# Latent attention of one Trainium2 kernel: from bf16 stacks of parts to fp32 strips of 32 partitions

## The reference, cut to what matters

```python
D_MODEL, N_HEADS, N_KV, HEAD_DIM, D_LAT = (128, 8, 2, 128, 32)
scale = HEAD_DIM ** (-0.5)
q = (x @ wq).reshape(Bq, Tq, N_KV, N_REP, HEAD_DIM)
k_lat = (x @ wk_down).reshape(Bq, Tq, N_KV, D_LAT)
v_lat = (x @ wv_down).reshape(Bq, Tq, N_KV, D_LAT)
k = jnp.einsum('bkhl,ld->bkhd', k_lat, wk_up)
v = jnp.einsum('bkhl,ld->bkhd', v_lat, wv_up)
scores = jnp.einsum('bqhrd,bkhd->bhrqk', q, k) * scale
scores = jnp.where(causal, scores, jnp.finfo(scores.dtype).min)
probs = jax.nn.softmax(scores, axis=-1)
y = jnp.einsum('bhrqk,bkhd->bqhrd', probs, v)
return y.reshape(Bq, Tq, N_HEADS * HEAD_DIM) @ wo
```

## Time and profile before

| what | us |
|---|---|
| runs of the kernel | 1942.96, 1944.66, 1948.3 |
| median | 1944.66 |
| profiled execution, span | 1933.1 |
| PE busy | 1601.7 (83%) |
| DVE busy | 1180.5 (61%) |
| POOL busy | 818.4 (42%) |
| ACT busy | 786.5 (41%) |
| latent stage, from first projection to last add | 1362.5 to 1846.6 |

### The profile page before, as it was taken

How to read it: one execution, slowest core, us unless ns; L and a number is a source line. 1 busy time by engine, 2 the same in 40 slices (tenths; PEclk the granted TensorE clock), 3 DMA queues, 4 the chain that set the end, 5 groups by cost and what they waited for, 6 DMA issues and landing times.

```text
span 1933.1 us, 25832 instructions
## 1 busy us (share of the span) xinstructions
PE 1601.7 (83%) x8863; PEld 807.4 (42%) x8863; DVE 1180.5 (61%) x2315; ACT 786.5 (41%) x1031; POOL 818.4 (42%) x987
## 2 busy tenths in 40 slices
PE   4766699758999899999799789989545898988779
PEld 2222466412333333332466567766212333333256
DVE  5887633578788787883333333342355878897951
ACT  2222233343565565667333344444212343334433
POOL 2224646464554635455463644000001577456900
PEclk8788699867999999999799999979656898889979
DMA  4000000151000303000000000000143000000000
GB/s 139 1 0 0 1 1 0 59 121 29 2 2 12 41 3 51 2 2 1 1 1 0 0 1 0 0 1 0 49 117 96 1 1 1 1 1 1 1 1 22
DMA packets 31585, 36.86 MB, mean 19 GB/s; under 512 B 8606, under 2 KB 24703, under 8 KB 31362
## 3 DMA queue, kind: packets, MB, share of 16 engines
q1 hardware_dynamic: 27906, 29.29, 6.4%
q10 hardware_dynamic: 3520, 6.29, 1.6%
q0 software_dynamic: 64, 0.00, 0.0%
HBM read 26.10 MB, written 8.91 MB: 18 GB/s over the span
## 4 chain that ended last, share of the span: by engine, by line
PE 61%; DVE 16%; DMA 7%; SPq 3%; issue 2%; ACT 2%; ACTq 0%; DVEq 0%
PE PS L943 9%; PE PS L1355 9%; PE PS L931 9%; PE PS L1304 8%; PE PS L1374 8%; DVE sb_latent_acc L1462 3%; DMA sb_rope_K<-rope_parts 3%; PE PS L1723 3%; PE PS L1741 3%; SPq L1629 2%; DVE sb_latent_mp L1538 2%; DMA latent_parts<-sb_latent_parts 2%; DVE sb_rope_mp L1538 2%; DVE sb_latent_rec L1568 1%; PE PS L1735 1%
## 5 line engine op out<-in xcount | busy, mean ns | idle before, releaser
L1538 DVE TENSOR_REDUCE sb_rope_mp<-PS 128x1 f32<-128x512 f32 (+3 forms) x560 | 345.0, 669 | 76.5 <-PE PS L1308 36.9
L1418 ACT ACTIVATE sb_rope_PT<-PS 128x1024 f32<-128x1024 f32 (+3 forms) x320 | 273.3, 895 | 223.0 <-PE PS L1359 121.7
L1462 POOL TENSOR_TENSOR sb_latent_acc<-sb_latent_acc,sb_latent_PT 128x1536 f32<-128x1536 f32 (+3 forms) x72 | 223.2, 3101 | 72.4 <-ACT sb_latent_PT L1418 68.8
L1418 ACT ACTIVATE sb_latent_PT<-PS 128x1024 f32<-128x1024 f32 (+3 forms) x160 | 140.2, 895 | 243.3 <-PE PS L1359 80.9
L995 DVE SCALAR_TENSOR_TENSOR sb_X<-PS,sb_gates,sb_X 128x128 f32 (+1 forms) x320 | 90.1, 344 | 241.3 <-PE PS L943 241.2
L1304 PE MATMUL PS<-sb_rope_K,sb_rope_Q 96*128 96x512 bf16 (+3 forms) x640 | 211.7, 371 | 30.2 <-ACT sb_rope_V L1399 18.3
L1538 DVE TENSOR_REDUCE sb_latent_mp<-PS 128x1 f32<-128x512 f32 (+3 forms) x280 | 174.3, 666 | 46.2 <-PE PS L1304 32.5
L576 POOL TENSOR_SCALAR sb_pbelow<-sb_pa,sb_ptrial 128x512 f32<-128x512 f32 x124 | 197.0, 1599 | 6.4
L583 POOL TENSOR_TENSOR sb_pbelow<-sb_pbelow 128x1024 f32<-128x1024 f32 (+1 forms) x248 | 181.7, 733 | 19.6
L931 PE MATMUL PS<-sb_HT,sb_w 128*128 (+1 forms) x384 | 182.3, 612 | 3.6 <-DVE sb_seed L514 1.9
L1355 PE MATMUL PS<-sb_rope_Q,sb_rope_K 99*128 99x512 bf16 (+3 forms) x640 | 179.4, 352 | 1.4 <-ACT sb_rope_PT L1418 0.9
(11 more groups left out here) (291 smaller groups left out, 2438.7 us busy)
## 6 DMA issues: line engine op xcount, KB each, us to landing
latent_parts<-sb_latent_parts SPq DMA_DIRECT2D x36, 128.0 KB
sb_rope_Q<-rope_parts SPq DMA_DIRECT2D x9, 384.0 KB
rope_parts<-sb_rope_parts SPq DMA_DIRECT2D x24, 128.0 KB, 2.4
sb_rope_tab<-in_rotation SPq DMA_DIRECT2D x1, 2048.0 KB, 8.6
sb_rope_K<-rope_parts SPq DMA_DIRECT2D x6, 256.0 KB
sb_latent_Q<-latent_parts ACTq DMA_DIRECT2D x2, 768.0 KB
sb_latent_Q<-latent_parts SPq DMA_DIRECT2D x1, 1536.0 KB, 19.1
sb_rope_Q<-rope_parts ACTq DMA_DIRECT2D x6, 192.0 KB
```

The costliest lines, as they stand in the source:

```text
L1418: s.activation(self.PT[:, u % 2, 2 * p:2 * p + 2, q0:CH], k.PS[:, 2 * p:2 * p + 2, q0:CH], ACT.Exp, scale=self.scale).then_inc(self.exps[p ...
L1462: eng.tensor_tensor(acc, acc, new, ALU.add).then_inc(self.added[who], 1)
L1538: v.tensor_reduce(self.mp[:, n % 2, kc, heads[0]:heads[-1] + 1, i], k.PS[:, bank, 0:len(heads) * w].rearrange("p (h k) -> p h k", h=len(he ...
```

## The change

A new stage `StripHeads` replaces `CausalHeads` for latent attention; rotary attention keeps the old one.

- The four heads of a quad lie on partitions 0, 32, 64, 96 (32 rows each: a strip) of Q and K, which are fp32. The projection itself puts them there: for K by weights repeated four times (`wkrep`, made by two POOL copies in LaterWeights). There are four projections per chunk. ACT copies Q, DVE copies K. No parts, no constants, no scratch tensor and no load remain.
- Scores and maxima are fp32 matmuls over the 32 rows of a strip. An item of maxima is one head (320 items in place of 280), in the order of strips 2, 3, 0, 1. Masks stay bf16 over all rows and come first. The negated maxima are added by a bf16 matmul of ones with three rows of each strip.
- POOL splits the negated maxima, PE turns them with four transposes, ACT copies them into negT. No DMA.
- The chunk is the outer loop, the quad the inner one. The rate is 5.0, without a steady share.
- PT has three buffers, acc two. Of the units of a chunk every third (kj = 0, 3, 6, ...) has its row sums made by PE (item "part", four matmuls into a ring bank, added to S by DVE), the others are added by POOL alone, all four heads in one instruction of up to 2048 columns.
- At the chunk end PE sums acc, DVE adds it to S; a DMA gathers the four rows into 128 x 16, DVE takes the reciprocal, a DMA puts it back, PE spreads it over each strip ("den"), DVE multiplies, PE projects, DVE adds.
- The constants grow by 128 columns.

The core of the diff:

```diff
+        for i in range(2):
+            g.tensor_copy(k.wkrep[:, i, :, :], k.wkv[:, 0, 32 * i:32 * i + 32].rearrange("p (a l) -> p a l", a=1)
+                          .broadcast_to([P, 4, 32])).then_inc(self.ready, 1)
...
+class StripHeads(Stage):
...
+    R = 3
+    AHEAD = 3
+    PTS = 3
+    NQ = 2
+    NS = 3
+    D = 32
...
+        self.seq = [(c, g) for c in range(NC) for g in range(self.NQ)]
+        self.units = [(n, kj) for n, (c, g) in enumerate(self.seq) for kj in range((c + 1) * TPC)]
+        self.first = [self.units.index((n, 0)) for n in range(len(self.seq))] + [len(self.units)]
...
+    def pe_sums(self, kj):
+        return kj % 3 == 0
+    def chunk_maxima(self, n):
+        c, g = self.seq[n]
+        return [("max", n, i, kc, j) for i in range(TPC) for kc in range(c + 1) for j in (2, 3, 0, 1)]
...
+            late = max(min(d, np.ceil(d - self.rate * max(0, first - self.AHEAD - u))) for first, d in due)
+            return int(min(len(items), max(late, 0)))
...
+            rests[end + 2].append(("sum", n))
+            relays[end + 5].append(("reciprocals", n))
+            rests[end + 7].append(("den", n))
+            rests[end + 8].append(("out", n))
...
+            a, b = (len(mine) + 3) // 4, (len(mine) + 1) // 2
+            if u < total:
+                plan.append((u, "scores0"))
+            plan += ring(mine[:a])
+            if u < total:
+                plan.append((u, "scores1"))
+            plan += ring(mine[a:b])
+            if 1 <= u <= total:
+                if self.pe_sums(self.units[u - 1][1]):
+                    plan.append((None, ("part", u - 1)))
+                plan.append((u - 1, "weighted"))
+            plan += [(u, it) for it in relays[u]]
+            plan += ring(mine[b:])
+            for it in rests[u]:
+                if it[0] == "turn":
+                    plan.append((u, ("split", it[1])))
+                plan.append((None, it))
+        return plan
...
+    def pe_scores(self, pe, u, p):
+        k = self.k
+        n, c, g, kj, q0 = self.unit(u)
+        if p == 0 and kj == 0:
+            self.emptied(pe, ("turn", n))
+        if u:
+            pe.wait_ge(self.exps[p], u)
+        diag = kj >= c * TPC
+        pair = (2 * p, 2 * p + 1)
+        if diag:
+            for j in pair:
+                pe.matmul(k.PS[:, j, q0:q0 + P], k.identb[:, :], k.mask_kq[:, :], start=True, stop=False,
+                          skip_group_check=True)
+        for j in pair:
+            strip = slice(32 * j, 32 * j + 32)
+            pe.matmul(k.PS[:, j, q0:CH], self.K[strip, g, kj * P:(kj + 1) * P],
+                      self.Q[strip, g, c * CH + q0:(c + 1) * CH], start=not diag, stop=False, skip_group_check=True)
+        for j in pair:
+            rows = slice(32 * j, 32 * j + 3)
+            pe.matmul(k.PS[:, j, q0:CH], k.onesb[rows, :], self.negT[rows, n % 2, q0:CH], start=False, stop=True,
+                      skip_group_check=True).then_inc(self.scores[p], 1)
+    def pe_weighted(self, pe, u):
+        k = self.k
+        n, c, g, kj, q0 = self.unit(u)
+        if kj == 0 and n:
+            pe.wait_ge(self.moved, n)
+        for p in range(2):
+            pe.wait_ge(self.exps[p], u + 1)
+        for j in range(4):
+            ins = pe.matmul(k.PS[32 * j:32 * j + 32, 4, q0:CH], self.V[:, kj, g, :], self.PT[:, u % self.PTS, j, q0:CH],
+                            start=(kj == 0), stop=(kj == (c + 1) * TPC - 1))
+        ins.then_inc(self.weighted, 1)
+    def pe_item(self, pe, item, bank):
+        k, kind = self.k, item[0]
+        if kind == "max":
+            _, n, i, kc, j = item
+            c, g = self.seq[n]
+            strip = slice(32 * j, 32 * j + 32)
+            w = CH if kc < c else (i + 1) * P
+            q0 = c * CH + i * P
+            if kc == c:
+                pe.matmul(k.PS[:, bank, w - P:w], k.identb[:, :], k.mask_qk[:, :], start=True, stop=False,
+                          skip_group_check=True)
+            return pe.matmul(k.PS[:, bank, 0:w], self.Q[strip, g, q0:q0 + P], self.K[strip, g, kc * CH:kc * CH + w],
+                             start=kc < c, stop=True, skip_group_check=True)
...
+        if kind == "part":
+            u = item[1]
+            n, c, g, kj, q0 = self.unit(u)
+            for p in range(2):
+                pe.wait_ge(self.exps[p], u + 1)
+            for j in range(4):
+                ins = pe.matmul(k.PS[32 * j:32 * j + 32, bank, q0:CH], k.ones_col, self.PT[:, u % self.PTS, j, q0:CH],
+                                start=True, stop=True)
+            return ins
...
+    def act_exps(self, s, u):
+        k = self.k
+        n, c, g, kj, q0 = self.unit(u)
+        if u >= self.PTS:
+            s.wait_ge(self.weighted, u - self.PTS + 1)
+            s.wait_ge(self.added, self.pool_adds(u - self.PTS + 1))
+        for p in range(2):
+            s.wait_ge(self.scores[p], 2 * (u + 1))
+            s.activation(self.PT[:, u % self.PTS, 2 * p:2 * p + 2, q0:CH], k.PS[:, 2 * p:2 * p + 2, q0:CH], ACT.Exp,
+                         scale=self.scale).then_inc(self.exps[p], 1)
...
+    def pool_add(self, g, u):
+        n, c, quad, kj, q0 = self.unit(u)
+        if self.pe_sums(kj):
+            return
+        if kj == 1 and n >= 2:
+            self.filled(g, ("sum", n - 2))
+        if self.pool_adds(u):
+            g.wait_ge(self.added, self.pool_adds(u))
+        for p in range(2):
+            g.wait_ge(self.exps[p], u + 1)
+        new, acc = self.PT[:, u % self.PTS, :, q0:CH], self.acc[:, n % 2, :, q0:CH]
+        if kj == 1:
+            g.tensor_copy(acc, new).then_inc(self.added, 1)
+        else:
+            g.tensor_tensor(acc, acc, new, ALU.add).then_inc(self.added, 1)
+    def pool_split(self, g, ch, n):
+        part = lambda r: self.negp[:, n % 2, :, :].rearrange("p i (j r) -> p i j r", r=32)[:, :, :, r]
+        neg, rest = self.neg[:, n % 2, :, :], self.rest[:, n % 2, :, :]
+        g.wait_ge(self.zeroed, 1)
+        g.wait_ge(self.negated, n + 1)
+        if n >= 2:
+            self.filled(g, ("turn", n - 2))
+        ch(g.tensor_copy(part(0), neg))
+        ch(g.tensor_tensor(rest, neg, part(0), ALU.subtract))
+        ch(g.tensor_copy(part(1), rest))
+        g.tensor_tensor(part(2), rest, part(1), ALU.subtract).then_inc(self.neg_split, 1)
...
+            a = StripHeads(k, "latent", ln, 5.0)
```

More of the change, by code:

```diff
@@ L98, in __init__ @@
         self.den_rope = self.cst[:, 3 * P:4 * P]
+        self.den_strip = self.cst[:, 15 * P:16 * P]
         self.ones_col = self.cst[:, 4 * P:4 * P + 32]
@@ L116, in bank @@
         return self.PS[:, b, 0:cols]
-N_CST = 5 + 8 + 2
+N_CST = 5 + 8 + 2 + 1
 class NormMemory:
@@ L290, in __init__ @@
         k.wc = sb("wc", [P, 8, 32])
+        k.wkrep = sb("wkrep", [P, 2, 4, 32])
         k.wy = sb("wy", [P, 2, P])
@@ L447, in tensor @@
         pe.wait_ge(s.ready, 1)
-        pe.wait_ge(self.ready, 4)
+        pe.wait_ge(self.ready, 6)
         n = 0
@@ L1881, in constants @@
     c[:, 14 * P:15 * P] = np.where(r[:, None] > r[None, :], MASKED, 0.0)
+    c[:, 15 * P:16 * P] = (r[:, None] // 32 == r[None, :] // 32) & (r[:, None] % 32 == 0)
     c[:, CST_ORDER:] = 8 - np.arange(8)
@@ L1987, in latent_attention @@
             ln = norm()
-            qb = [(0, 0, 0, 2), (0, 64, 0, 1), (1, 0, 0, 3)]
-            kb = [(0, 0, 0, 1), (0, 32, 0, 2), (1, 0, 2, 1), (1, 32, 1, 1), (1, 64, 0, 1)]
-            sources = [(k.wc[:, 4 * g:4 * g + 4, :].rearrange("p h l -> p (h l)"), None) for g in range(2)]
-            a = CausalHeads(k, "latent", ln, 2, sources + [(k.wkv[:, :, :].rearrange("p a l -> p (a l)"), None)], (qb, kb), 96, 1,
-                            k.wkv[:, 1, :], 2, 32, float(P ** -0.5), k.wy, d["latent_parts"], False, True, 4.5)
+            a = StripHeads(k, "latent", ln, 5.0)
             with ExitStack() as arena:
@@ L2042, in scratch @@
     d["rope_parts"] = nc.dram_tensor("rope_parts", (2, 16, 3 * 8, T), BF16).ap()
-    d["latent_parts"] = nc.dram_tensor("latent_parts", (3, 4, 3 * 32, T), BF16).ap()
 def kernel(**inputs):
```

284 lines of the change are left out of this document (added).

## The result

The kernel after takes 2154.09 us (median of four runs, 2127.62 to 2165.42), the kernel before 1946.24 us beside it: ratio 1.1018, 95% interval 1.0944 to 1.1092. The ratio and its interval are of the fast executions, without the slowest of the four after. The forecast was 1916, with a range up to 1995. The profiled execution after took 2127.62 us, the lowest of the four, span 2125.6.

The account below looks back on a forecast made before the run. It took TensorE, gapless in mid-stage units, and 111 us of preparing as the bound. First scores at 1413 plus 392 gave 1805, closing 12.5 gave 1817.5, 29 us earlier: 1944.66 - 29 + 0.3 = 1916 us, range 1860 to 1995.

Parts of the forecast that it names:

- a granted clock of 0.5 in the strips: Strip products: listed sign that the forecast is wrong; the forecast itself expected clock 0.9 at the first scores.
- the rival of 1945 us: Whole stage: preparation 48 us shorter, middle 48 us longer (full unit 5.7 us, missed handovers and lower clock); chance 0.06.
- the sum: Stage from first scores to last units: full units with maxima 5.0 us, diagonal ones, chunk ends, last units; together 392 us.
- Preparation: Before first scores: parts and reloads go, maxima begin at 1383.7 us, first scores at 1413 instead of 1473.6.
- Do strips overlap?: Score products on row strips: a pair of heads overlaps, 0.86 us, 1.07 with negated maxima; 2.13 without overlap.
- The rival of no overlap, 2197 us: Row strips never overlap: a full unit takes 9.9 us, 281 us added; chance 0.12.
- Products start only one after the other: Rival on strip products: no half passes a waiting one, full unit 6.05 instead of 5.0 us, total 1981; chance 0.15.
- VectorE and GpSimd: Beside TensorE in full units: GpSimd adds of 2048 columns 4.6 us, reductions 0.69 us each, both hidden.
- full units have maxima waiting for reductions: Full units: three banks fill, so the fourth maximum waits for the first's VectorE reduction, to 1.8 us; unit 5.0.
- The last units: Units without maxima at the stage's end: 3.2 us each, set by GpSimd and handover.
- The end: After the last weighted group: closing steps take 12.5 us, against 10.5 before.
- 60 us gained: Preparation: first scores at 1413 us instead of 1473.6; bounds 48 to 70 us.

Follow-up runs that it names:

- e6: Kernel after with only the diagonal blocks' maxima taken over all 128 rows instead of one strip, masks kept (values not the reference's): 1962.29 us.
- e5: Kernel after without the mask products before the diagonal maxima: 1933.03 us (ten runs), ratio to before 0.9936.
- e3: Kernel after with VectorE reducing only 128 columns of each maximum: 2149.1 us.
- e1: Kernel after with all maxima over 128 rows instead of a 32-row strip (values are sums over four heads): 2053.37 us.
- e4: Kernel after with maxima taken from bf16 copies of Q and K, one pass instead of two, scores still fp32: 1926.91 us, ratio to before 0.988.
- e9: Kernel after reordered only: where two diagonal maxima follow each other, both masks are issued first, then both products: 2071.2 us.
- e10: e4 (bf16 maxima) with the order of e9 (masks issued in pairs): 1885.48 us, ratio to before 0.9705.
- e7: e4 (bf16 maxima) without the masks before the maxima: 1839.04 us, ratio to before 0.9464.
- e11: e7 with the planner's rate 6.0 in place of 5.0, six maxima a unit: 1865.09 us, ratio to before 0.9602.
- e12: Kernel after with masks left out of the 39 maxima up front alone: 2146.39 us (two runs), ratio to before 1.1047.
- e2: Kernel after with one further full-array bf16 matmul of 128 x 512 before each maximum: 2537.27 us.

## Why the prediction was wrong

The direction was wrong, and the step that failed is **the clock**. The text priced each strip product warm, put "a granted clock of 0.5 in the strips" on the list of what would show it wrong, and gave it no term; a lower clock stands only in the rival of 1945 us, as one of two reasons for 48 us, with a chance of 0.06. That there is a lower level was in the rows: the earlier trace rows have 0.58 for preparing, and a slow weighted group. I took both for TensorE being idle. Here TensorE hardly idles (0.65 of 577.8 us), and it still runs at the lower level for most of the time (0.69).

In numbers, from the first maximum to the first unit without one: after 1393.7 to 1971.5, 577.8 us; e6, the same list of instructions with the diagonal maxima on all rows, 1394.5 to 1806.4, 411.9 us. The clock is worth **166 us** in these two executions, a lower bound if anything: a diagonal maximum of after can still overlap with a score behind it, one of e6 cannot, and the other runs of after were 22 to 38 us longer than the profiled one. The forecast for this stretch was 367 (1383.7 to 1413, then 392 - 54), so **45 us** are wrong at full clock too. Up front is not where they come from (29.3 us forecast from first maximum to first scores; e6 has 26.7, 1394.5 to 1421.2). They lie mostly in units that hold diagonal maxima. In e6 a full unit without them took 4.94 us on average, 5.60 with row sums on TensorE (the forecast had 4.66 and 5.66); with one or more of them 6.44 and 6.68 (units with chunk-end work left out). In after a wide masked maximum takes 1.21 us at the upper clock; by the sum's own rule (0.86 for 512 columns, 0.06 for the mask, 0.12 for the changes of shape) it would be 1.04. It also ends the overlap of what stands before it, which the sum did not contain. e5, where masks are gone, needs 385.8 us for the stretch, 26 less than e6, in spite of its lower clock.

Point by point:
- *Preparation.* Right up to the first maximum, and wrong behind it. First maximum 19.7 us after the first projection (1374.0 to 1393.7; 21.2 forecast). The reloads and their 111 us are gone. But the first scores come 76.6 us after the first projection (1374.0 to 1450.6), against 51 forecast, at a clock of 0.52 where 0.9 was forecast. In e5, without masks, they come after 48.0 us (1371.4 to 1419.4), also at the low clock.
- *Do strips overlap?* Right: a pair in 1.13 us, and what follows a pair of maxima starts 1.06 us after it (1753.25 to 1754.31). The rival of no overlap, 2197 us, is nearest to the time measured and is wrong as to its cause. Its number was met by another mechanism.
- *Products start only one after the other.* Refuted: four halves in 1.13 us, a score and a maximum 0.01 us apart. Where nothing is masked even the four strips run together: eight halves of scores in 1.15 us (1997.71, in the last units of after). That starts and ends keep the order of the program does not forbid such an overlap, as the prediction took it to.
- *VectorE and GpSimd.* Right. The 2048-column adds take 4.52 us on average in after (4.6 forecast), a 512-column reduction still 0.69 us, and reductions hold nobody (e3). That full units have maxima waiting for reductions was wrong: TensorE waited for them 0.2 us in all.
- *The last units.* Right: 54.6 us for 17 spacings, 3.2 each.
- *The end.* Right: 2026.96, the last weighted group, to 2039.03, the end of the last add, is 12.1 us; 12.5 forecast.
- *60 us gained.* The term was sized at the upper clock. From the first projection to the first scores before took 111.1 us and after 76.6, so 34 were gained; the 39 maxima and what belongs to them took 56.9 us at 0.52 (1393.7 to 1450.6) and 26.7 at 1.00 in e6.

The Trainium skill ("TensorE: Matmul & The Clock Gate", Part 1, What's actually happening) says that the clock follows how busy TensorE has been, and under Why this matters for your kernels it advises to keep it continuously busy. The rows here disagree where the work is on strips: busy 60.00 of 60.00 us at a clock of 0.56. The page's other statement, that a product over 32 rows takes the time of one over 128, agrees: 592 ns is the median duration of the halves of e1's 512-column maxima over 128 rows, and 588 ns that of e5's on strips.

What stays open is which quantity the clock follows. The part up front, with the maxima on strips and no weighted group yet, had 0.51 to 0.54 in all ten kernels that kept its maxima on strips: one strip at a time (after, e3, e4), two (e9, e10), several (e5, e7, e11, e12), and also where a product over the whole array stands before each maximum (e2). In the units, where weighted groups over the whole array stand between, it was 1.00 with the lone diagonal maxima moved to 128 rows, 0.92 without masks, 0.64 to 0.72 with them, and 0.60 when every maximum was separated. That lone strips lower it fits these stretches of units, except that e9 has fewer of them and no higher clock; it does not fit the part up front of e5. e9's profile is of one execution, after itself shows 0.56 and 0.97 in windows of the same kind of units, and after and e3 differ by 0.05 over the whole stretch; I had no run that separates chance of this sort from a rule. What is shown is narrower: moving the diagonal maxima from 32 to 128 rows, or leaving out the masks before them, lifts the clock of the units.

## What to carry to other kernels

Price row-strip matmuls at both clocks: the two levels differ by a factor of two, more than the overlap of two strips gains (1.06 us for two products of 0.86), and a busy TensorE is no evidence for the higher one. Before splitting the array, list what stands between the strip products: a small matmul over all rows in front of each makes it run alone, and a mask that only shifts a maximum can be left out, as long as the masked scores are not so much larger than the others that the exponentials vanish (no run here tests that). Cut the strip work itself where precision allows (one bf16 pass for maxima that cancel out), and read the granted clock of the stretch before anything else.

## What was not expected of the hardware

- TensorE, busy for 75.89 of 76.3 us, ran at 0.52 up front with fp32 products over 32 rows (0.53 with bf16 ones, e4), and at 1.00 with the same maxima over 128 rows (e1).
- Added full-array bf16 products of 512 columns did not raise the clock; with one before each maximum it was 0.60 in the units, against 0.72.
- Leaving out 128 mask products (0.16 us from the start of each to that of its maximum, at the upper clock) made the kernel 221 us faster.
- The kernels with the lowest clocks in the units spread more from run to run: after 1.8% of the time, e4 1.8, e9 2.8, against 1.1 for e5 (ten runs), 0.7 for e7 and 0.3 for e10 and e11.
